# M accumulated row quarter by row quarter, x's first tile group with its own scale, and queries and values in pairs

## The reference

```python
q = x @ Wq.T + bq;  k = x @ Wk.T + bk;  v = x @ Wv.T + bv
a = q @ k.T / sqrt(512) + adj + adj
x = layernorm(x + softmax(a) @ v)
h = relu(adj @ (x @ W1) + b1)
x = layernorm(x + adj @ (h @ W2) + b2)
```

## Time and profile before

| | us |
|---|---|
| median of three runs | 1917.63 |
| the profiled execution | 1917.4 |
| its span | 1915.4 |
| TensorE busy | 1894.9 |
| VectorE busy | 1074.8 |
| ScalarE busy | 857.9 |
| first M pass | 8.58 |
| first fp16 matmul | 27.77 |
| first matmul of the scores | 185.87 |

### The profile page before, as it was taken

One profiled execution on the slowest core, in us unless ns is written; L12 is line 12 of the kernel. 1 busy time (PEld: TensorE's weight loads), 2 busy tenths in 40 slices (PEclk: granted clock), 3 DMA queues, 4 the chain that ended last, 5 costly groups with the idle time before them and its releaser, 6 DMA issues.

```text
span 1915.4 us, 26409 instructions
## 1 busy us (share of the span) xinstructions
PE 1894.9 (99%) x9252; PEld 885.7 (46%) x9252; DVE 1074.8 (56%) x2049; ACT 857.9 (45%) x1837; POOL 114.5 (6%) x207
## 2 busy tenths in 40 slices
PE   7999999999999999999999999999999999999998
PEld 3444444444444444444444444444444454444445
DVE  7875666666666666666666666666666620002334
ACT  5654464555555555555555555555445511011112
POOL 0000000000000000000000000000000000002334
PEclk9999999999999999999999999999999999999999
DMA  8563599999999999999999999999999999979996
GB/s 282 116 141 86 131 236 224 232 228 223 227 224 223 233 228 229 225 225 224 227 229 225 228 227 226 230 222 224 227 226 237 218 345 387 387 290 390 394 394 248
DMA packets 799526, 465.29 MB, mean 243 GB/s; under 512 B 644641, under 2 KB 652321, under 8 KB 799137
## 3 DMA queue, kind: packets, MB, share of 16 engines
q1 hardware_dynamic: 789888, 446.82, 94.0%
q10 hardware_dynamic: 9504, 16.79, 2.4%
HBM read 223.09 MB, written 92.01 MB: 165 GB/s over the span
## 4 chain that ended last, share of the span: by engine, by line
PE 93%; DMA 2%; DVE 2%; issue 1%; POOL 1%; ACT 1%; SPq 0%; POOLq 0%; DVEq 0%; ACTq 0%
PE bank L526 14%; PE bank L528 14%; PE bank L527 14%; PE bank L621 11%; PE bank L623 11%; PE bank L622 11%; PE bank L739 5%; PE bank L740 5%; PE bank L738 5%; DMA tsp<-gT 1%; POOL tsp L1491 1%; DMA adj_in<-in_L_gnn_Wv 1%; DMA xv<-in_x 0%; DVE sc L1066 0%; DVE ring L1077 0%
## 5 line engine op out<-in xcount | busy, mean ns | idle before, releaser
L879 ACT ACTIVATE tsp<-ring,sc 128x512 f16<-128x512 f32 x249 | 179.7, 722 | 601.5 <-DMA tsp<-tsp 600.8
L1246 DVE SCALAR_TENSOR_TENSOR ring<-bank,sc,adj_in 128x512 f32<-128x512 f32 x256 | 192.2, 751 | 389.2 <-PE bank L528 383.7
L621 PE MATMUL bank<-xv,tsp 128*128 128x512 f16 x1024 | 388.1, 379 | 1.8 <-DMA tsp<-gT 1.8
L526 PE MATMUL bank<-xT,gT 128*128 128x512 f16 x1024 | 388.1, 379 | 0.0
L527 PE MATMUL bank<-xT,gT 128*128 128x512 f16 x1024 | 388.1, 379 | 0.0
L528 PE MATMUL bank<-xT,gT 128*128 128x512 f16 x1024 | 388.1, 379 | 0.0
L622 PE MATMUL bank<-xv,tsp 128*128 128x512 f16 x1024 | 388.1, 379 | 0.0
L623 PE MATMUL bank<-xv,tsp 128*128 128x512 f16 x1024 | 388.1, 379 | 0.0
L1077 DVE SCALAR_TENSOR_TENSOR tsp<-adj_in,s_a,tsp 128x512 f16<-128x512 f32 x248 | 184.8, 745 | 53.9 <-ACT tsp L887 53.2
L1077 DVE SCALAR_TENSOR_TENSOR tsp<-ring,sc,tsp 128x512 f16<-128x512 f32 x249 | 185.7, 746 | 2.6 <-ACT tsp L879 2.6
L869 ACT ACTIVATE ring<-ring,bias 128x512 f32<-128x512 f32 x256 | 180.9, 707 | 8.8 <-DVE bias L1263 8.8
(11 more groups left out here) (224 smaller groups left out, 2124.5 us busy)
## 6 DMA issues: line engine op xcount, KB each, us to landing
xv<-at_dram SPq DMA_DIRECT2D x66, 1024.0 KB, 11.6
adj_in<-in_adj SPq DMA_DIRECT2D x256, 256.0 KB, 3.4
at_dram<-tsp SPq DMA_DIRECT2D x248, 256.0 KB, 3.2
xT<-at_dram SPq DMA_DIRECT2D x21, 1024.0 KB, 16.3
adj_in<-at_dram SPq DMA_DIRECT2D x18, 1024.0 KB, 11.1
xv<-in_x SPq DMA_DIRECT2D x8, 1024.0 KB, 11.2
g_dram<-tsp SPq DMA_DIRECT2D x32, 256.0 KB, 3.7
gT<-g_dram SPq DMA_DIRECT2D x32, 256.0 KB, 3.7
```

The source lines that it names most:

```text
L526: pe.matmul(dst, ah, bh, start=(i == 0), stop=False)
L621: pe.matmul(dst, ah, vh, start=(kb == 0 and j == 0), stop=False)
L879: act.activation(p_split(e)[:, 0:BANK], p, ACT.Copy, scale=col[f"p_up{batch(TW * kb)}"]).then_inc(a_p, 1)
L1246: dve.scalar_tensor_tensor(t, s_bank[s % S_BANKS][:, :], col[f"k_l{batch(s // KB)}{batch(TW * (s % KB))}"], adj_in[:, s % AR, :], ALU.mult ...
```

## The change

- Wq and Wk are loaded in two steps each: row quarter 0 of both first, then the rest; then x group 0, Wv, x group 1. bv and x groups 2 to 4 are issued after the transposes of tiles 0 to 3; groups 5, 6 and 7 one by one behind the transposes of tiles 4, 5 and 6.
- M is summed over e in the outer loop and over the four banks in the inner one, from the first quarters on.
- x has three scales: tiles 0 to 3, 4 to 7, and the rest (`batch`). The group sums are all whole groups on ScalarE, and POOL reduces each scale by itself. Two of bq's partial products go to ScalarE and are summed in TensorE's accumulation (12 small products for 4).
- Wv's maximum is taken in four pieces, and its split comes after M's.
- TensorE runs two queries, then two values. Queries of group g follow no longer four tiles behind: both `queries(4g)` and `values(4g)` wait for all four transposes of group g. There are two banks for values.
- `x_tiles_at(t)` names two tiles at the first and two at the second t of each group, for the next group; tiles 8 to 11 all at t = 5. `store_g(t//4-1)` is at every fourth t from 4 on.

```diff
 def batch(t):
-    return 0 if t < FIRST else 1
+    return min(t // XG, BATCHES - 1)
 def x_tiles_at(t):
-    if t < FIRST - 3:
-        return [t + XS + 1] if t + XS + 1 < FIRST else []
...
+    g, i = divmod(t, XG)
+    first = XG * (g + 1)
+    if first >= NT or i > 1:
+        return []
+    if first == FIRST:
+        return [[], list(range(first, first + XG))][i]
+    return [first + 2 * i, first + 2 * i + 1]
...
+            sp.dma_start(wq_raw[:, 0:1, :], wq_rows[:, 0:1, :]).then_inc(d_w0, 16)
+            sp.dma_start(wk_raw[:, 0:1, :], wk_rows[:, 0:1, :]).then_inc(d_w0, 16)
+            sp.dma_start(wq_raw[:, 1:KD, :], wq_rows[:, 1:KD, :]).then_inc(d_wr, 16)
+            sp.dma_start(wk_raw[:, 1:KD, :], wk_rows[:, 1:KD, :]).then_inc(d_wr, 16)
...
+            load_x(0)
+            sp.dma_start(wv_raw, wv.rearrange("(k p) d -> p k d", p=P)).then_inc(d_wv, 16)
+            load_x(1)
...
             for t in range(XS):
                 transpose_x(t)
-            load_x(SP_GROUPS)
-            transpose_x(XS)
-            for i in range(SP_GROUPS + 1, NT // XG - 1):
+            sp.dma_start(bv_row, bv.rearrange("(o d) -> o d", o=1).broadcast_to([P, D])).then_inc(d_bv, 16)
+            for i in range(X_FIRST, X_FIRST + 3):
                 load_x(i)
             for t in range(NT):
                 for q in x_tiles_at(t):
                     transpose_x(q)
-                if t == 0:
-                    load_x(NT // XG - 1)
+                    if X_FIRST + 3 + q - XG < NT // XG:
+                        load_x(X_FIRST + 3 + q - XG)
...
-                if t % XG == 0 and t >= 2 * XG:
-                    store_g(t // XG - 2)
+                if t % XG == 0 and t >= XG:
+                    store_g(t // XG - 1)
...
+            pe.wait_ge(d_w0, 16 * 2)
+            for e in range(KD):
+                if e == 1:
+                    pe.wait_ge(d_wr, 16 * 2)
+                for k in range(KD):
+                    last = pe.matmul(m_bank[k][:, :], wq_raw[:, e, P * k:P * (k + 1)], wk_raw[:, e, :],
+                                     start=(e == 0), stop=(e == KD - 1))
...
             def values(t):
-                pe.wait_ge(d_xt[t % XS], 16 * (t // XS + 1))
...
+                if t % XG == 0:
+                    for i in range(XS):
+                        pe.wait_ge(d_xt[i], 16 * (t // XG + 1))
...
-            for t in range(NT):
+            for t in range(0, NT, 2):
+                if t < NT - XG:
+                    queries(t)
+                    queries(t + 1)
                 values(t)
-                if t >= XG:
-                    queries(t - XG)
+                values(t + 1)
...
             dve.wait_ge(d_small, 16 * 2)
-            dve.wait_ge(d_wq, 16)
...
+            partial(part_u, wq_raw, bk_c, range(KD))
+            partial(part_g[2], wk_raw, bq_c, range(2, KD))
...
+            wv_max(0)
             x_scale(0)
+            wv_max(1)
             xt_lo(0)
             xt_lo(1)
...
+            m_max(0)
             xt_lo(2)
+            m_max(1)
+            xt_lo(3)
+            m_max(2)
+            m_max(3)
+            dve.tensor_reduce(col["st_m"], cols("m0", "m3"), AX, ALU.max).then_inc(v_st, 1)
...
+            for k in range(KD):
+                m_lo(k)
+            dve.wait_ge(g_ar, 5)
+            power(col["e_wv"], col["mx_wv"])
+            scale_of(col["s_wv"], col["e_wv"]).then_inc(v_sc, 1)
+            dve.wait_ge(v_sc, 1)
+            for k in range(KD):
+                wv_lo(k)
+            dve.wait_ge(g_ar, 4)
+            g_scale(0)
+            dve.wait_ge(d_bv, 16)
+            link(abs_max(col["mx_bv"], bv_row))
+            v_scale(0)
+            x_scale(1)
...
             for t in range(NT):
-                if t == FIRST:
-                    v_scale(1)
+                if t in BATCH_STARTS[1:]:
+                    v_scale(batch(t))
+                if t % 2 == 0 and t < NT - XG:
+                    g_lo(t)
+                    g_lo(t + 1)
                 v_full(t)
...
+            pool.wait_ge(a_xs, 1)
+            pool.partition_all_reduce(col["mx_x0"], x_sum[:, 0:1], P, ALL_MAX).then_inc(g_ar, 1)
```

More of the change, by code:

```diff
@@ L24 @@
 FIRST = XG * X_FIRST
-SP_GROUPS = 4
+BATCHES = 3
+BATCH_STARTS = (0, XG, FIRST)
 KB = N // BANK
@@ L523, in _, with terms @@
         def _(pe):
+            def terms(dst, ah, al, bh, bl, first, last):
+                pe.matmul(dst, ah, bh, start=first, stop=False)
+                pe.matmul(dst, ah, bl, start=False, stop=False)
+                return pe.matmul(dst, al, bh, start=False, stop=last)
             def product(dst, pairs):
                 for i, (ah, al, bh, bl) in enumerate(pairs):
-                    pe.matmul(dst, ah, bh, start=(i == 0), stop=False)
-                    pe.matmul(dst, ah, bl, start=False, stop=False)
@@ L528, in product @@
-                    last = pe.matmul(dst, al, bh, start=False, stop=(i == len(pairs) - 1))
-                return last
[L531 to L551, removed]
+                    last = terms(dst, ah, al, bh, bl, i == 0, i == len(pairs) - 1)
+                return last
+            def wv_transposes(j):
+                for k in range(KD):
+                    last = pe.transpose(wv_bank[j][:, P * k:P * (k + 1)], wv_raw[:, k, P * j:P * (j + 1)], ident)
+                last.then_inc(p_wv, 1)
@@ L555, in _ @@
             for k in range(KD):
-                last = pe.matmul(bank[6][:, k:k + 1], part_g[:, P * k:P * (k + 1)], ones[:, 0:1], start=True, stop=True)
+                for i, part in enumerate(part_g):
+                    last = pe.matmul(bank[6][:, k:k + 1], part[:, P * k:P * (k + 1)], ones[:, 0:1],
+                                     start=(i == 0), stop=(i == len(part_g) - 1))
             last.then_inc(p_pre, 1)
@@ L836, in _ @@
                 m_hi(k)
+            act.wait_ge(v_sc, 1)
+            for k in range(KD):
+                wv_hi(k)
+            group_sum(2)
             for t in range(NT):
+                if t % 2 == 0 and t < NT - XG:
+                    g_hi(t)
+                    g_hi(t + 1)
                 v_hi(t)
@@ L1077, in minus_hi, with partial, wv_max, m_max @@
                 return dve.scalar_tensor_tensor(dst, src, scale, hi, ALU.mult, ALU.subtract)
[L1080 to L1083, removed]
+            def partial(dst, rows, weight, rows_of):
+                first, *between, end = rows_of
+                link(dve.tensor_scalar(dst, rows[:, first, :], weight[:, first:first + 1], None, ALU.mult))
+                for e in between:
                     link(dve.scalar_tensor_tensor(dst, rows[:, e, :], weight[:, e:e + 1], dst, ALU.mult, ALU.add))
[L1085 to L1091, removed]
+                dve.scalar_tensor_tensor(dst, rows[:, end, :], weight[:, end:end + 1], dst, ALU.mult, ALU.add).then_inc(v_part, 1)
+            def wv_max(k):
+                link(abs_max(col[f"w{k}"], wv_raw[:, k, :]))
+            def m_max(k):
+                dve.wait_ge(p_pre, k + 1)
+                link(abs_max(col[f"m{k}"], m_bank[k][:, :]))
             def wv_lo(k):
```

193 lines of the change are left out of this document (78 added, 115 removed), and 3 rows, old and new, of the table names.

## The result

The changed kernel took **1946.94 us**, the median of four runs (1945.2 to 1948.6), against 1916.98 for the kernel before: a ratio of 1.0148 on record, with an interval of 1.0136 to 1.0160 (the quotient of these two medians is 1.0156). It is 28 to 30 us slower. Forecast were 21.3 us and a range of 1926 to 1946. The time lies at the upper edge of that range: the ratio times the 1917.63 us from which the forecast started gives 1946.0, and the median itself passes the edge by 0.9.

A forecast was written before the change was run, and what follows sets the result against it. The prediction took TensorE (busy 99% of the span) as the bound; first logits at 56.8 + 135.2 + 1.7 + 1.5 + 12.0 = 207.2 against 185.87, a shift of +21.3 on 1917.6, gave 1939 us, range 1926 to 1946.

The forecast's parts named there:

- queries(4) starts at: Second group of tiles: transpose 7 lands at 56.8 us (bounds 54.5 to 59), so PE waits 9.7 us.
- half rate after it: After the 9.7 us wait at queries(4), matmuls restart at half rate, 1.7 us lost (bounds 0 and 3).
- wait at queries(8), start to start: Third group: tiles 8 to 11 all come at t=5, landing 22.3 us after queries(4) starts against a need at 20.8: +1.5 us.
- five waits behind stores, start to start: Groups at t=8 to 24: transposes issued behind a store make PE wait 2.4 us in each of five groups, 12.0 us.
- The start of the queries: M runs from 4.7 to 20.3 us with four slow passes; queries(0) starts at 26.3+0.4 against 27.77, gain 1.1 us.
- The queue behind tile 4: SP's queue alternates transposes 4 to 7 with loads; group 5 goes into an idle queue (5.2 us), transpose 7 lands at 56.8.
- The later groups: From t=8, a store between two transpose pairs delays the second pair; +12 us, bounds 0.6 to 3.0 for each group.
- Rival E: Each of the five 2.4 us waits also drops the clock, 1.7 us each, 8.5 more: 1947.5; chance 0.08.
- What costs nothing: Two value banks, added small VectorE operations, whole group sums on ACT, removed first-logits wait and earlier group 6 store add no time.
- Rival A: Transposes pass the loads: transpose 7 lands at 50.1, with no slow restart: 1930.5; chance 0.12.
- rival B: Stores don't hold the transposes back: five waits of 0.6 us, 9 us less, 1930; chance 0.12.
- Rival D: Not slower: tiles 4 to 7 land before 47.1 and later groups' in time, first logits 3.2 us early: 1914.5; chance 0.08.

The follow-up runs named there:

- e1: Changed kernel with the loads of x groups 5 to 7 issued right behind groups 2 to 4, ahead of tile 4's transpose: 1940.53 us.
- e2: Changed kernel with stores of query groups 1 to 6 and the first gT load issued behind the second pair of transposes: 1933.74 us.
- e3: Changed kernel with both moves, loads of x ahead and stores behind the second pair of transposes: 1925.91 us.
- e7: Changed kernel with TensorE's old order, values(t) then queries(t-4), each values(t) waiting for tile t alone; loads, transposes and splits left as they are: 1924.34 us.
- e5: e3 with tiles 8 to 11 spread over t = 4 and 5, group sums a step earlier, small operations moved to t = 18: 1923.76 us.
- e8: Changed kernel with 46 extra fp16 matmuls into an unused bank ahead of queries(4), filling the wait: 1943.9 us.
- e10: Changed kernel with bq's partial sums in one piece on VectorE, 8 one-column matmuls in place of 24: 1946.2 us.
- e4: Kernel before with only the first row quarters of Wq and Wk loaded first and M summed by row quarter: 1917.48 us against 1918.01.
- e9: e4 with the load of x group 4 issued ahead of the transposes of tiles 0 to 3: 1915.55 us against 1917.85.
- e6: e5 with ScalarE's M hi parts ahead of the c_row copy and the last Wv transposes behind queries(1): 1923.65 us.

## Why the prediction was right, and where it was short

**The mechanism held.** Seven waits, at the places named: one of 10.9 us at the fifth query, one of 1.9 at queries(8), five behind stores. e1 and e2 removed the first and four of the five by changing only the order of issue, e3 showed them to be separate, and e7 showed the third part, that the slack spent by the new order of products is what made them cost. No term has the wrong sign; each of the first five is too small, so the errors added up, and with them the time came out at the edge of the range.

**The size was short by 10.2 us** (first logits at 217.4 in place of 207.2). By the terms of the sum, in the profiled execution:

| term | forecast | measured |
|---|---|---|
| queries(4) starts at | 56.8 | 60.9 |
| half rate after it | 1.7 | 2.4 |
| wait at queries(8), start to start | 1.5 | 2.1 |
| five waits behind stores, start to start | 12.0 | 14.0 |
| half rate after these | 0 | 3.4 |
| 52 products | 135.2 | 134.6 |

*The start of the queries* carries 2.5 of the 4.1 us in the first line: 29.16 against 26.7. It began with M (22.1 against 20.3): the first pass started at 5.21 and not 4.7, and seven passes were 0.85 us apart, not four. Then c_row's two matmuls at half rate, which weren't in the sum at all, held up ScalarE's `m_hi` (27.38), and the gap on TensorE in which the 16 small matmuls were to lie wasn't there. But e1, e2, e3, e5 and e8 have the same code for TensorE up to here, and queries(0) began at 26.76, 27.67, 29.20, 26.74 and 30.34, with c_row's pair at full rate in e1, e2 and e5 and at half rate in e3 and e8. In e1 and e5 M took 15.4 and 15.5 us, where the forecast had 15.6 and the changed kernel took 16.9. So the 26.7 of the forecast was met in two executions of six, and it had no term for the rate at which the start would run.

*The queue behind tile 4* carries 1.7 us, and these come again where the start was early: from queries(0) to queries(4) it is 31.8 us in the changed kernel and in e2, 32.0 in e10, against 30.1 in the forecast. Tile 4's transpose was issued 15.0 us after the start, not 14.5. From there to tile 7's landing the queue took 16.6 us, where I had 15.6: I had let group 5's load go into an idle queue (5.2 us), but tile 4's transpose was ahead of it, and it landed 6.4 us after its issue. Two small slips in the text of the prediction move nothing: 3x1.2+2x2.8 is 9.2, not 9.1, and with queries(0) at 26.7 PE would have stood idle from 47.5 on, not 47.1.

*The later groups.* From one late wait's end to the next it was 24.0, 25.4, 23.6, 23.2 and 23.1 us, against 23.2 in the forecast: the last two steps came as summed. In the first, the first pair took 3.47 us to issue in place of 2.6, so the store came 14.6 us after the group's start, not 13.6; tile 15 then landed 109.9-100.64=9.3 us after it, against 9.6 taken from the earlier trace rows. The second holds a stretch at half rate (1.7 us) and the load of gT between store and transpose, the third the 16 small operations of t = 16: the two cases for which the prediction had set its bound of 3.0.

*Rival E* was half right. Two of the five waits (3.12 and 2.21 us) were followed by matmuls at half rate, 1.7 us each, where it had five times 1.7. I had argued from a single row that a wait of 2.4 us leaves the rate as it is. One example wasn't enough.

*What costs nothing.* Two value banks and the whole group sums on ScalarE: no wait of the changed kernel names the banks (in e7 two do, 1.6 us). The group sums weren't free once the long wait was gone (e1, e3: 2.6 us more at queries(8)).

*Rival A* (transposes pass the loads) fell with the landings of 6.7 to 8.3 us and with e1, *rival B* (or the stores) with tile 15's landing and with e2. *Rival D* named the conditions well: with both moves made (e3) and the third group spread (e5) the kernel comes to 5.3 us above the one before, not below it. What is left there are 7.4 us of waits.

**Open.** In e5's profiled execution (1921.97 us) no wait was followed by half rate, and the first logits came at 190.19, 4.3 us after the kernel before: 7.4 us of waits against 1.8, less 1.0 for the earlier start. Why the median of ten is another 1.8 us above that execution isn't shown. Which wait is followed by a stretch at half rate stays open as well (below).

## What to carry to other kernels

When an order of work is changed so that a consumer needs its operands a few steps sooner, count the slack that the old order had and list everything that sits ahead of the producer on its queue: a 1 MB load was worth 2.8 to 3.4 us (from one transpose's landing to the next load's, tiles 5 to 7) and a store of four queries about 4.8 us of lateness here (9.3 us from its issue to the second landing, where two transposes alone take 1.3+3.2), and in the kernel before these had cost at most its two waits of 0.9 us. Starting the first engine earlier is worth nothing while another chain (x's split, scale and transpose) ends at the same place. And issue the transfer that the critical engine waits for before those that merely have to be done.

## What the runs showed of the hardware

- After each of the six waits for transposed tiles or splits of 4.0 us and more (4.0 in e7 to 11.0 in e10), matmuls came at half rate, 0.43 us apart, the lower level of 1.2 GHz. Shorter waits aren't ordered by their length: 1.7 (e4), 2.0 (e9 and e10), 2.1 (e2), 2.2 and 3.1 (changed kernel) and 3.5 us (e6) were followed by half rate; 2.0 and 3.1 (e8), 2.7 and 2.8 (changed kernel) and 3.8 us (e5) were not. The granted clock over stretches of the changed kernel, third column from the right:

```profile
20.00:30.00 10.00, 10.00 (x53) 7.20 (x53) 7.93 (x20) 3.62 (x7) 1.53 (x4) 0.83 0.84 199
30.00:40.00 10.00, 10.00 (x48) 4.55 (x47) 8.45 (x32) 7.02 (x10) 0.00 (x0) 1.00 0.63 233
...
61.00:66.00 5.00, 5.00 (x13) 1.76 (x14) 0.00 (x0) 0.00 (x0) 0.00 (x0) 0.53 1.20 304
...
110.00:114.00 4.00, 3.92 (x11) 1.52 (x12) 0.00 (x0) 0.00 (x0) 0.00 (x0) 0.57 0.00 0
```

- Half rate also came with no wait at all: from 24.8 to 28 us PE is busy without a gap and runs at half rate (granted clock 0.50), behind 24 matmuls of one column. With the same code it came in the profiled executions of the changed kernel, e3 and e8 and not in those of e1, e2 and e5.
- A stretch at half rate behind a wait cost 1.4 to 2.9 us each time (1.4 in e10, 2.9 in e1), about as much as a short wait itself.
- The slow passes at the start aren't a fixed number: with the same code for TensorE, the 32 passes of M took 15.4 us in e1, 15.5 in e5 and 16.9 in the changed kernel.
